# Cross attention with layer norm on one core: xt and residual loads issued by ScalarE, and steps within a slot moved

## The reference

```python
Q = split_heads(query @ Wq + bq)
K = split_heads(key @ Wk + bk)
V = split_heads(value @ Wv + bv)
scores = jnp.einsum('bhqd,bhkd->bhqk', Q, K) / np.sqrt(D_K)
attn = jax.nn.softmax(scores, axis=-1)
ctx = jnp.einsum('bhqk,bhkd->bhqd', attn, V)
out = ctx.transpose(0, 2, 1, 3).reshape(B, S, D_MODEL) @ Wo + bo
return _layer_norm(out + query, ln_gamma, ln_beta)
```

## Time and profile before

| | |
|---|---|
| median of 3 executions | 716.09 us (712.96 to 720.47) |
| profiled execution, its time | 716.47 us |
| profiled execution, span | 714.7 us |
| mean granted TensorE clock | 0.966 |
| TensorE, VectorE, GpSimd, ScalarE busy | 631.0, 544.0, 450.4, 365.8 us |
| DMA queue of SP: share of 16 engines' span | 69.1% |

### The profile page before, as it was taken

The page is one execution under the profiler, slowest core; times in us unless marked ns, Lnnn a source line. Parts: engine busy times, 40 slices in busy tenths (PEclk is TensorE's granted clock), DMA queues, the critical chain, the costliest instruction groups (busy, mean ns, idle before and its releaser), DMA issues.

```text
span 714.7 us, 12042 instructions
## 1 busy us (share of the span) xinstructions
PE 631.0 (88%) x3336; PEld 430.6 (60%) x3336; DVE 544.0 (76%) x971; ACT 365.8 (51%) x667; POOL 450.4 (63%) x399
## 2 busy tenths in 40 slices
PE   6988967989898899999999989899989998998791
PEld 5966644666565656565665666566656565665470
DVE  4543265869797788888888888898889887887766
ACT  4611044456465566555656656565556565654541
POOL 1421023457676677776776777677767677765697
PEclk9999996999999999999999999999999999998996
DMA  9763567576777777778777776878677767675712
GB/s 321 283 203 84 148 175 181 146 167 172 185 190 179 187 181 188 190 183 199 197 173 194 177 194 180 212 186 201 178 191 190 193 186 190 170 174 146 213 60 88
DMA packets 93393, 129.58 MB, mean 181 GB/s; under 512 B 49937, under 2 KB 49937, under 8 KB 93361
## 3 DMA queue, kind: packets, MB, share of 16 engines
q1 hardware_dynamic: 93360, 129.19, 69.1%
HBM read 53.94 MB, written 24.35 MB: 110 GB/s over the span
## 4 chain that ended last, share of the span: by engine, by line
SPq 32%; PE 15%; DMA 12%; DVE 11%; issue 10%; POOL 8%; ACT 4%; ACTq 0%; DVEq 0%; POOLq 0%
SPq L539 18%; DMA xt<-in_x_t 10%; SPq L517 8%; PE p_o L658 5%; DVE part L811 4%; PE p_q L594 3%; SPq L475 3%; ACT qh L731 2%; DVE ql L860 2%; POOL y L961 2%; DMA xn<-in_x 2%; PE p_a L610 2%; POOL y L965 2%; PE p_s L624 2%; PE p_o L98 2%
## 5 line engine op out<-in xcount | busy, mean ns | idle before, releaser
L716 ACT ACTIVATE prob<-p_s 77x512 f32<-77x512 f32 x256 | 143.3, 586 | 50.5 <-PE p_s L624 48.7
L811 DVE TRANSPOSE_TENSOR_REDUCE part<-prob 96x64 f32<-96x2048 f32 x64 | 146.9, 2296 | 1.2 <-ACT prob L716 1.1
L868 DVE TENSOR_REDUCE nm<-p_a 128x4 f32<-128x308 f32 x256 | 115.7, 474 | 34.8 <-PE p_a L610 28.5
L610 PE MATMUL p_a<-kb,qh 128*128 128x308 f32 x256 | 86.2, 340 | 32.4 <-ACT qh L731 23.6
L951 POOL TENSOR_TENSOR xl<-xt,xh 128x512 fp32r<-128x512 f32 x60 | 77.2, 1287 | 58.8 <-ACT xh L723 58.8
L970 POOL TENSOR_TENSOR cl<-cxt,ch 128x512 fp32r<-128x512 f32 x64 | 82.5, 1289 | 47.4 <-ACT ch L741 47.4
L961 POOL TENSOR_TENSOR y<-y,gamma_row 128x512 f32<-128x512 f32 x60 | 76.6, 1276 | 52.5 <-ACT y L753 52.5
L977 POOL TENSOR_TENSOR xn<-xn,bo_row 128x512 f32<-128x512 f32 x60 | 77.4, 1290 | 45.1 <-DMA xn<-in_x 45.1
L624 PE MATMUL p_s<-z,ks 97*77 97x512 f32 x256 | 98.5, 426 | 7.6 <-issue 5.9
L594 PE MATMUL p_q<-xh,wqh 128*128 128x512 f32 x256 | 102.4, 400 | 1.7 <-PEq L150 1.7
L594 PE MATMUL p_q<-xl,wqh 128*128 128x512 f32 x256 | 102.2, 399 | 0.0
(11 more groups left out here) (123 smaller groups left out, 994.8 us busy)
## 6 DMA issues: line engine op xcount, KB each, us to landing
z<-qh SPq DMA_DIRECT2D x256, 128.0 KB, 2.3
xt<-in_x_t SPq DMA_DIRECT2D x64, 256.0 KB, 3.6
z<-ql SPq DMA_DIRECT2D x128, 128.0 KB, 2.3
xn<-in_x SPq DMA_DIRECT2D x60, 256.0 KB, 3.2
out_dram<-y SPq DMA_DIRECT2D x60, 256.0 KB, 3.3
ks<-k_high SPq DMA_DIRECT2D x32, 154.0 KB, 3.6
cx<-in_ctx_t SPq DMA_DIRECT2D x4, 616.0 KB, 5.4
k_high<-kth SPq DMA_DIRECT2D x4, 616.0 KB, 3.6
```

What stands on the lines that cost most here:

```text
L610: nc.tensor.matmul(p_a[t % 2][:, 0:HC * S2], qh[:, g.k // 2 % 2, g.k % 2, P * t:P * (t + 1)], kb[g.k // NCH % 2][:, g.k % NCH, :], start=T ...
L716: nc.scalar.activation(prob[0:S2, j, :], p_s[j % 2][0:S2, :], ACT.Exp, scale=SCALE).then_inc(prob_ready, 1)
L811: nc.vector.tensor_reduce(part[:], prob[0:KP, :, :].rearrange("p h (i r) -> p (h i) r", r=DK), AX_X, ALU.add, apply_transpose=True).then_i ...
L868: nc.vector.tensor_reduce(nm[:, t, g.k % 2:HALF:2], p_a[t % 2][:, 0:HC * S2].rearrange("p (h k) -> p h k", k=S2), AX_X, ALU.max, negate=Tr ...
```

## The change

The loads of xt (chunk g+5) and of the residual tile (g-7) are issued by ScalarE instead of SP. ScalarE's `split_x_high` moves from the start of its slot to its end, followed by the xt load. Normalizing (`minus_mean_over_std` on VectorE, `normalize` on ScalarE) is done one slot later, and on VectorE it stands behind `sum_keys` and not at the slot's end. `scale` and `shift` are one slot later too, while the store stays where it was in lag, and in SP's slot it now stands ahead of z. GpSimd's `ctx_low` goes ahead of `inverse_std`. The drain at the end follows suit.

```diff
@@ -42,7 +42,8 @@
 LAG_PV = 4
 LAG_OUT = 8
 LAG_NORM = 9
-LAG_SCALE = 10
+LAG_NORMALIZE = 10
+LAG_SCALE = 11
 LAG_STORE = 11
 WO_SLOTS = (3, 5)
 
@@ -527,8 +528,8 @@
                     if g.back(1).is_first():
                         sp.wait_ge(kb1_zeroed, 1)
                     load_kb(g.back(1 - NCH))
-                if g.back(LAG_LOAD_X).valid(NG):
-                    load_xt(g.back(LAG_LOAD_X))
+                if g.back(LAG_STORE).valid(NS):
+                    store(g.back(LAG_STORE))
                 if g.k % 2 == 1 and g.back(1).valid(NG):
                     c = g.back(1)
                     i = c.k // 2 % 2
@@ -538,13 +539,6 @@
                         for j in range(HC):
                             sp.dma_start(z[DK * part:DK * (part + 1), i, j, :, :].bitcast(F32),
                                          src[DK * j:DK * (j + 1), i, :, :].bitcast(F32)).then_inc(z_in[i], 16)
-                m = g.back(LAG_NORM - 2)
-                if m.valid(NS):
-                    if m.is_first():
-                        sp.wait_ge(wo_low, KC)
-                        sp.wait_ge(wo_high, KC)
-                    all_at_least(sp, (squared, m.over(1, -1)))
-                    sp.dma_start(xn[:, m.k % 2, :], x_dram[m.over(1)]).then_inc(xn_in[m.k % 2], 16)
                 if last_batch_chunk(g, 1) == NCH - 2:
                     for t in range(QT):
                         if t == 0:
@@ -553,8 +547,6 @@
                         if t == 2:
                             sp.wait_ge(pv_summed, NG - NCH)
                         sp.dma_start(x_last[t], x_dram[NS + t]).then_inc(x_last_in[t], 16)
-                if g.back(LAG_STORE).valid(NS):
-                    store(g.back(LAG_STORE))
                 for i in v_in_slot(g.back(1)):
                     store_v(i)
                 if g.back(WO_SLOTS[0]).is_first():
@@ -747,6 +739,19 @@
                 nc.scalar.activation(xn[:, m.k % 2, :], y[:, i, :], ACT.Square, bias=nmean[:, i, :],
                                      accum_out=ssd[:, i, :]).then_inc(squared, 1)
 
+            def load_residual(m):
+
+                if m.is_first():
+                    act.wait_ge(wo_low, KC)
+                    act.wait_ge(wo_high, KC)
+                all_at_least(act, (squared, m.over(1, -1)))
+                act.dma_start(xn[:, m.k % 2, :], x_dram[m.over(1)]).then_inc(xn_in[m.k % 2], 16)
+
+            def load_xt(n):
+
+                all_at_least(act, (xh_ready, n.over(1, -1)), (xl_ready, n.over(1, -1)))
+                act.dma_start(xt[:, n.k % 2, :], xt_dram[n.over(1)]).then_inc(xt_in[n.k % 2], 16)
+
             def normalize(m):
                 i = m.k % 4
                 act.wait_ge(nmr_ready, m.over(1, 1))
@@ -762,24 +767,29 @@
 
             def slot(g):
                 s, v, m, n = g.back(LAG_SCORE), g.back(LAG_PV), g.back(LAG_NORM), g.back(LAG_SPLIT)
-                if n.valid(NG):
-                    split_x_high(n)
                 if g.valid(NG):
                     q_high(g)
                 if m.valid(NS):
                     square(m)
+                if g.back(LAG_NORM - 2).valid(NS):
+                    load_residual(g.back(LAG_NORM - 2))
                 if s.valid(NG):
                     for j in range(HC):
                         exp(s, j)
                 if v.valid(NG):
                     ctx_high(v)
-                if m.valid(NS):
-                    normalize(m)
+                if g.back(LAG_NORMALIZE).valid(NS):
+                    normalize(g.back(LAG_NORMALIZE))
+                if n.valid(NG):
+                    split_x_high(n)
+                if g.back(LAG_LOAD_X).valid(NG):
+                    load_xt(g.back(LAG_LOAD_X))
                 for kc in wo_in_slot(g):
                     split_wo_high(kc)
             run(act, slot)
+            normalize(Slot(0, NS - 2))
             square(Slot(0, NS - 1))
-            for m in range(NG + LAG_PV - LAG_NORM, NS + ON_POOL):
+            for m in range(NS - 1, NS + ON_POOL):
                 normalize(Slot(0, m))
 
         @block.vector
@@ -880,6 +890,8 @@
                 v, m = g.back(LAG_PV), g.back(LAG_NORM)
                 if v.valid(NG):
                     sum_keys(v)
+                if g.back(LAG_NORMALIZE).valid(NS):
+                    minus_mean_over_std(g.back(LAG_NORMALIZE))
                 if m.valid(NS):
                     add_residual(m)
                 if g.valid(NG):
@@ -894,8 +906,6 @@
                         row_maxima(g, t)
                     if g.k % 2 == 1:
                         turn_maxima(g)
-                if m.valid(NS):
-                    minus_mean_over_std(m)
                 for i in v_in_slot(g):
                     dve.wait_ge(v_summed, i + 1)
                     dve.wait_ge(v_stored[i % 4], 16 * (i // 4))
@@ -927,6 +937,7 @@
                                                op0=ALU.mult, op1=ALU.add).then_inc(y_last_done, 1)
 
             m = Slot(0, NS - 1)
+            minus_mean_over_std(Slot(0, NS - 2))
             add_residual(m)
             variance_of_squares(m)
             add_last(0)
@@ -989,10 +1000,10 @@
                     split_x_low(n)
                 if b.valid(NS):
                     add_bo(b)
+                if v.valid(NG):
+                    ctx_low(v)
                 if m.valid(NS):
                     inverse_std(m)
-                if v.valid(NG):
-                    ctx_low(v)
                 t = last_batch_chunk(g, LAG_PV + 1)
                 if t is not None:
                     add_bo_last(t)
@@ -1003,20 +1014,22 @@
             run(pool, slot)
             add_bo_last(QT - 1)
 
-            last = [Slot(0, NS + t) for t in range(-2, QT)]
+            last = {t: Slot(0, NS + t) for t in range(-3, QT)}
+            scale(last[-3])
+            shift(last[-3])
+            inverse_std(last[-1])
+            scale(last[-2])
+            shift(last[-2])
+            inverse_std(last[0])
+            scale(last[-1])
+            inverse_std(last[1])
+            shift(last[-1])
+            inverse_std(last[2])
             scale(last[0])
-            inverse_std(last[1])
+            inverse_std(last[3])
             shift(last[0])
-            inverse_std(last[2])
             scale(last[1])
-            inverse_std(last[3])
             shift(last[1])
-            inverse_std(last[4])
-            scale(last[2])
-            inverse_std(last[5])
-            shift(last[2])
-            scale(last[3])
-            shift(last[3])
 
 
 def xattn(nc, a, out):
```

## The result

The changed kernel takes 928.6 us (median of 4, 927.55 to 929.55) against 718.3 for the kernel before in the same comparison: ratio 1.294, 95% interval 1.285 to 1.303. It is slower, as forecast, but by 210 us and not by 21; the range ended at 760.

The account below looks back on a forecast made before the run. It took a batch-long circle through SP's store, z and maxima to bind: 37.5 plus clock 1.7 and residual issue 0.4 makes 39.6 us against 37.9. Times 13 adds 22, less 1: 716.5 becomes 737 us, range 702 to 760.

Parts of the forecast that it names:

- The new place of nmr: VectorE, nmr between part and the residual addition: no net cost, 0 us a slot, bounds -0.8 and +0.8.
- The store ahead of z: SP's odd slot: the store waits for y_done, 8.9 us after the slot's start, and holds z, maxima and later scores.
- the circle over a batch: From scores(4j) to scores(4j+4) through stall, y_done, store, z and maxima: 37.5 us, 39.6 with clock and residual issue.
- A new stall at each batch: TensorE waits for the batch's last xh and xl before slot 4j: 3.2 us in each of 15 batches, bounds 2.5 and 3.5.
- The clock: TensorE's granted clock falls after the stall before slot 4j: 1.7 us a batch, bounds 0 and 3.5.
- ScalarE's two issues: On ScalarE, xt's issue costs nothing; the residual's, before the exponentials, 0.4 us in one slot a batch, bounds 0 and 1.
- What goes: ScalarE's 2.6 us xt delay in slots 4j+1, GpSimd's residual wait, and some 1.4 us of SP issues in two slots.
- A: Rival: the batch circle is looser and the removals win, 37.0 us a batch, 703 us; chance 0.22.
- B: Rival: the boundary stall takes what the xt wait gave back, 37.9 us a batch, 716 us; chance 0.13.
- C: Rival: SP's row maxima land after 4.0 us, the batch circle grows to 41.3 us, 760 us; chance 0.17.
- What would show it: Signs for right: no xt wait, 3 us stall before p_q, lower clock, SP waiting, TensorE idle before p_s, 39-40 us batch.

Follow-up runs that it names:

- e1: The changed kernel with GpSimd's split_x_low moved to the end of its slot, behind add_bo, ctx_low and inverse_std: 754.7 us, 1.050 of the kernel before.
- e3: The changed kernel with VectorE's nmr moved from between part and the residual addition to behind variance_of_squares: 766.3 us.
- e2: The changed kernel with SP's store of row tile g-11 put back behind the z issues: 927.8 us.
- e7: The kernel of e5 with SP's store put back behind z: 716.1 us, against 720.2 for e5.
- e9: The kernel of e5 with nmr behind variance_of_squares and ScalarE's residual load behind the four exponentials: 666.7 us, 0.932 of the kernel before.
- e5: The changed kernel with ScalarE's split_x_high back at its slot's start and the xt load behind the residual load: 720.2 us, 1.002 of the kernel before.
- e10: The changed kernel with nmr behind variance_of_squares, xh between second and third exponential, both loads behind the fourth, GpSimd's xl behind add_bo: 662.5 us, 0.925 of before.
- e11: The kernel of e5 with nmr behind variance_of_squares and both loads issued by SP again: 726.0 us, 1.013 of the kernel before.
- e4: The changed kernel in its order, with the xt and residual loads issued by SP again: 925.3 us.

## Why the prediction was wrong, point by point

- *The new place of nmr* is the step that failed. It said that nmr "no longer waits for rstd in front of part" and took 0, bounds -0.8 and +0.8 us a slot. In the changed kernel nmr waited for rstd 53 times, 144 us in all, and with it y, TensorE's p_o and square. The working was at hand: under *The store ahead of z* I followed GpSimd's slot from xh to y_done (xh ends 1.7 us past the boundary, y_done comes 7.2 later), and passed over the two results on the way that VectorE needs at the head of its next slot, xn 2.6 us and rstd 4.3 us behind xh. With them, nmr ends 5.6 us behind xh, and another 8.6 lead back to xh. That is a ring of one slot, 14.15 us, where I looked for one of a batch. e1 cut it and took off 174 us; e3 took cl, rstd and nmr out of it and took off 162.
- *The store ahead of z* and the circle over a batch: y_done came about as late as I said (8.5 us past the boundary of slot 33, 8.9 forecast) and SP waited 370 us for it, but it never bound (e2: -1 us; e7: -4), and TensorE had no idle time before p_s that z could explain (2.8 us in all). The circle of 37.5 us was shorter than four turns of the ring.
- *A new stall at each batch*: right. 3.2 us was forecast; e1 shows 3.33, and in the changed kernel itself it is 2.7 (40.6 over 15), inside the bounds.
- *The clock*: right in kind, too small. 1.7 us a batch was taken; e1's clock stood at 0.50 to 0.57 for 6 us behind the stall, 2.9 us of loss by the windows. The nearest kernel that has the stall and its clock without the ring is e1, 755 us against the 737 forecast. In the changed kernel the clock fell behind every gap of a batch: 0.50 in slots 33 and 34, 0.57 in slot 35 (496 to 500) and 0.65 behind the boundary stall (504 to 508).
- *ScalarE's two issues*: the xt issue at the slot's end costs nothing, as said. For the residual one 0.4 us was taken; the gap in front of the exponentials is 0.75 in the changed kernel, and e9 gained 0.45 us a slot without it. I had written that this issue waits for its own square, and priced the issue but not the wait. I charged it in one slot of four, while it stands in each.
- *What goes*: ScalarE's wait for xt and GpSimd's for xn went, as said.
- Rivals: A, B and C all had one batch-long circle in mind. None was a ring within one slot.
- *What would show it*: most of the signs named for being right came true (no wait for xt, a stall of 2.7 us before p_q, a clock of 0.842, SP waiting for y), although the circle that they were to show didn't bind. Only the batch of 53.9 us and the missing idle time before p_s spoke against it. That slower was right owes something to the stall and its clock, which e1 still has at 755 us, and nothing to the store.

What stays open: the 0.6% between e5 and e7 was not looked into, and how the clock's share of the 210 us would stand by itself was not tried; it is argued from e3 and the windows. GpSimd's new order alone was not tried either: it puts cl, 1.27 us, in front of rstd, and so into each turn of the ring.

## What to carry to other kernels

When a step is moved to the end of an in-order engine's slot, list everything queued behind its consumer on the consumer's engine, and for each result ask which slot's head needs it; add up the ring back to the moved step before any longer circle. A transfer issued by a compute engine belongs where that engine waits anyway, behind the instructions that others wait for; look first at what the issue itself waits for, above all a result of the same engine that is still being made. Moving loads to another queue is worth what the old queue delayed them, and only if the new place isn't in front of something that binds.

## What the runs showed that I had not expected

- An issue on ScalarE is listed with 0.34 us, but one that waited for ScalarE's own square left it idle for 0.75 us (changed kernel), and with a second issue behind it for 1.27 to 1.70 (e5). Issues with nothing to wait for are made while ScalarE computes: in e9 xt was issued at 373.24, while square ran, and in e1 at 409.89, before ctx_high, which stands ahead of it in the code, began at 410.19.
- A TensorE gap of 3.33 us was followed at once by a clock of 0.50 for 4 us and 0.57 for 2 more (e1; it had begun to fall inside the gap, 0.72 at 412 to 414), against full speed for 2 us and 0.57 for 4 behind the gap of 2.47. The loss belongs in the sum with the gap: here 2.9 us for 3.3.
- With ScalarE issuing loads z's transfers took longer to land: 3.6 us median in the changed kernel and 4.2 in e10, against 2.3 before and 2.3 in e11, where SP issued all. But e4, where SP issued all too, has 3.0, so the cause is not shown. e10 is the fastest kernel all the same.
